# Set-up and plan moved into the mixer block, x loaded by halves, one stage order per engine, and a last stage that adds by DMA

## The reference, cut to what matters

```python
x = x + _layernorm(_L0_attn_ref(_layernorm(x), ...))
x = x + _layernorm(_L0_ffn_ref(_layernorm(x), ...))

# mixer
x = _lin(x, w1); x = silu(_depthwise_conv(x, conv_w, conv_b))
x_delta = softplus(_lin(x, dl_w, dl_b))
A_bar = exp(-x_delta * _lin(x, A_w, A_b))
A_cum = cumprod(A_bar, axis=1)
h = cumsum(_lin(x, B_w, B_b) * A_cum, axis=1)
ssm_out = _lin(h, C_w, C_b) + _lin(x, D_w, D_b)
out = ssm_out + _lin(ssm_out * silu(_lin(ssm_out, w2)), w3)

# ffn: top 2 of 8 experts for each token, and a shared one
probs = softmax(xn @ router_w); topv, topi = top_k(probs, 2)
for e in range(8):
    out = out + comb[:, e:e + 1] * _swiglu(xn, gate_up_w[e], down_w[e])
out = out + _swiglu(xn, shared_gate_up_w, shared_down_w)
```

## Time and profile before

| | us |
|---|---|
| median of 3 runs | 1341.65 |
| lowest and highest | 1341.48, 1345.4 |
| the profiled execution's own time | 1347.18 |
| its span in the trace | 1345.2 |
| PE, DVE, ACT, POOL busy | 1131.8, 858.6, 636.2, 310.0 |

### The profile page before, as it was taken

One profiled execution on the slowest core, in us unless ns is written; L12 is line 12 of the kernel. 1 busy time (PEld: TensorE's weight loads), 2 busy tenths in 40 slices (PEclk: granted clock), 3 DMA queues, 4 the chain that ended last, 5 costly groups with the idle time before them and its releaser, 6 DMA issues. The chain is left out here.

```text
span 1345.2 us, 23563 instructions
## 1 busy us (share of the span) xinstructions
PE 1131.8 (84%) x7568; PEld 998.5 (74%) x7568; DVE 858.6 (64%) x2158; ACT 636.2 (47%) x1275; POOL 310.0 (23%) x378
## 2 busy tenths in 40 slices
PE   1587888887897889829899999999999999999930
PEld 1365566665665646518899999999999999999930
DVE  3497589579868862515466666666666666666636
ACT  3545655555565433404344444444444444444414
POOL 2022025225322521320111111111111111111124
PEclk9798999899898989869999999999999999999975
DMA  5654647557474732235946811611111166211135
GB/s 184 220 186 157 225 155 247 180 181 265 154 244 153 248 118 67 87 145 227 320 110 214 331 31 31 219 31 28 28 24 30 31 212 208 48 31 31 31 93 172
DMA packets 96553, 191.71 MB, mean 143 GB/s; under 512 B 8704, under 2 KB 59392, under 8 KB 96512
## 3 DMA queue, kind: packets, MB, share of 16 engines
q1 hardware_dynamic: 82208, 172.48, 37.2%
...
## 5 line engine op out<-in xcount | busy, mean ns | idle before, releaser
L1162 PE MATMUL gu_ps<-xg_hi,w_ring 128*128 128x256 f32 x1248 | 356.8, 286 | 7.3 <-DMA w_ring<-w_split 7.3
L1164 PE MATMUL gu_ps<-xg_hi,w_ring 128*128 128x256 f32 x1248 | 348.4, 279 | 0.0
L1163 PE MATMUL gu_ps<-xg_lo,w_ring 128*128 128x256 f32 x1248 | 348.4, 279 | 0.0
L1134 POOL DMA_INDIRECT acc_scratch<-y,ids x78 | 127.3, 1633 | 587.0 <-DVE y L1234 560.7
L1255 DVE TENSOR_SCALAR gate<-gu_ps 128x256 f32<-128x256 f32 x312 | 132.1, 423 | 198.2 <-PE gu_ps L1164 198.2
L1215 ACT ACTIVATE gate<-gate 128x256 f32<-128x256 f32 x312 | 130.3, 418 | 243.1 <-DVE gate L1255 243.1
L1162 PEld LDWEIGHTS gu_ps<-xg_hi,w_ring 128*128 128x128 f32 x1248 | 236.1, 189 | 8.5 <-issue 5.7
L1163 PEld LDWEIGHTS gu_ps<-xg_lo,w_ring 128*128 128x128 f32 x1248 | 236.2, 189 | 0.0
L1164 PEld LDWEIGHTS gu_ps<-xg_hi,w_ring 128*128 128x128 f32 x1248 | 235.6, 189 | 0.0
L1207 ACT ACTIVATE hg_hi<-gate 128x256 fp32r<-128x256 f32 x312 | 129.9, 416 | 114.8 <-DVE gate L1262 114.8
L1173 PE MATMUL down_ps<-w_ring,hg_hi 128*128 128x256 f32 x624 | 175.3, 281 | 0.3 <-DVE hg_lo L1250 0.3
...
## 6 DMA issues: line engine op xcount, KB each, us to landing
...
```

The costliest lines, as they stand in the source:

```text
L1162: nc.tensor.matmul(out, e_hi[:, f, cols], xg_hi[:, par, c, :], start=c == 0, stop=False)
L1163: nc.tensor.matmul(out, e_hi[:, f, cols], xg_lo[:, par, c, :], start=False, stop=False)
L1164: i = nc.tensor.matmul(out, e_lo[:, f, cols], xg_hi[:, par, c, :], start=False, stop=c == DC - 1)
```

## The change

- The block `split_weights` is gone. Its loads, splits and constants are stages of `mixer`: p (weight splits), k (a bias sum), tab (tables on POOL). SP's queue begins with the two halves of x; the raw weights pass through the memory of `xnt`.
- x is loaded, measured, rooted and normalised by halves of 512 tokens (stages m, N), and the next batch's halves are loaded as soon as PE has transposed the last one's.
- Stages are cut finer: dl and A apart, scan into ac, bx and h, d 0 to 5 by output group on PE and ACT, the split of xs by channel half. The carries of both scans are copied by DVE where POOL did it.
- ORDER is now written out for all batches and the tail, word by word ("b6/1" is stage b of unit 6 in batch 1), for PE, ACT, DVE and POOL, and there is one for SP too. TAIL is gone. Six chunks of weights (w10 to w15 of the last batch) are split behind the last unit of that batch.
- The block `plan` is gone: its DVE instructions stand at the end of the mixer's DVE program, its eight clearing DMAs at the end of SP's.
- The block `finish` is gone: its stages stand at the end of `experts`. Behind group 2 SP copies x1 from DRAM to `out` in DRAM by four DMAs of 1 MB. At the end nobody adds on DVE: POOL issues for each chunk one DMA that adds the normalised 512 rows to `out` (accumulate).

```diff
-def split_weights(nc, weights, full, consts, w_hi, w_lo, w_full, vec, ident, zeros, ones, neg_half, tok_id, pad, tables):
...
-        @block.sync
-        def _(sp):
-            for n, (r, hi, lo, at, src, chunks) in enumerate(parts):
-                width = src.shape[1]
-                sp.dma_start(r[:, at:at + chunks * width].rearrange("p (c n) -> p c n", c=chunks),
-                             src.rearrange("(c p) n -> p c n", p=P)).then_inc(loaded[n], 16)
-            sp.dma_start(vec[:, :], consts).then_inc(vec_loaded, 16)
-            for at, src, chunks in full:
...
-def mixer(nc, x, w_e, w_s, shared, xs_dram, x1_dram, acc_dram, fill, w_hi, w_lo, w_full, vec, ident, tok_id, zeros, ones, neg_half):
+def mixer(nc, x, w_e, w_s, weights, full, consts, shared, xs_dram, x1_dram, acc_dram, fill, w_hi, w_lo, w_full, vec, ident,
+          tok_id, pad, zeros, ones, neg_half, tables, group_expert, group_change, group_row, group_code):
...
+        past = decay[:, 0, 0:(NG + 1) * E].rearrange("p (g e) -> p g e", e=E)
+        over = decay[:, 1, 0:E * MAXG].rearrange("p (e j) -> p e j", e=E)
+        unused, expert_f, passed_f, row_f = [decay[:, 1, (4 + i) * 48:(4 + i) * 48 + NG + 1] for i in range(4)]
...
+                "x0/1 n0/0 x1/1 n1/0 xr0/0 n2/0 n3/0 n4/0 spare/0 n5/0 n6/0 n7/0 n8/0 n9/0 n10/0 n11/0 n12/0 n13/0 n14/0 st0/0 "
...
-            def load_x(b):
-                sp.dma_start(x_in[:, :, :], x[b, :, :].rearrange("(t p) d -> p t d", p=P)).then_inc(x_loaded, 16)
+            def load_x(b, half):
+                sp.dma_start(x_in[:, half * HT:(half + 1) * HT, :], x[b, rows_of(half), :].rearrange("(t p) d -> p t d", p=P)
+                             ).then_inc(x_loaded[half], 16)
...
+            load_x(0, 0)
+            load_x(0, 1)
+            for n in range(2):
+                load_weights(raw_w, *weights[n], w_raw_loaded[n])
+            load_weights(w_full, *full[0], w_full_loaded[0])
+            sp.dma_start(vec[:, :], consts).then_inc(vec_loaded, 16)
+            for n in range(2, len(weights)):
+                load_weights(raw_w, *weights[n], w_raw_loaded[n])
+            for n in range(1, len(full)):
+                load_weights(w_full, *full[n], w_full_loaded[n])
             for at, src, chunks in shared:
                 sp.dma_start(w_sh[:, at:at + chunks * src.shape[1]].rearrange("p (c n) -> p c n", c=chunks),
                              src.rearrange("(c p) n -> p c n", p=P)).then_inc(w_sh_loaded, 16)
...
+            def spare_rows(b):
+                sp.wait_ge(consts_made, 2)
+                sp.dma_start(xs_dram[SPARE:SPARE + G, :].rearrange("(p m) d -> p (m d)", p=P), spare).then_inc(ends_cleared, 16)
+                sp.wait_ge(start_made, 1)
+                sp.dma_start(acc_dram[T:T + G, :].rearrange("(p m) d -> p (m d)", p=P), zeros[:, 0:GT * D]).then_inc(ends_cleared, 16)
+
+            def next_x(b, half):
+                passed(t1_done, (b - 1) * 4 + 2 * half + 2)
+                load_x(b, half)
+
...
+            def unit_product(b, n, at, bank, done):
+                half, j = UNITS[n]
+                cols = slice(half * HALF, (half + 1) * HALF)
+                if b == 0 and n == 0:
+                    pe.wait_ge(w_lo_ready, at // (DC * H) + 1)
+                for c in range(DC):
+                    if n == 0:
+                        pe.wait_ge(xs_lo_ready, b * DC + c + 1)
+                    i = product(banks[bank][:, :], W(w_hi, at, c, H, j * P), W(w_lo, at, c, H, j * P),
+                                xs_hi[:, c, cols], xs_lo[:, c, cols], c == 0, c == DC - 1)
+                i.then_inc(done, 1)
...
+            def x_moments(b, half):
+                tiles = slice(half * HT, (half + 1) * HT)
+                dve.wait_ge(x_loaded[half], b * 16 + 16)
+                moments(lambda t: x_in[:, half * HT + t, :], st[:, tiles, :], mv[:, tiles, :], HT, x_order, b * 2 + half + 1,
+                        a_aggr, b * 2 + half + 1, ve[:, tiles], 1.0, EPS, mv_ready)
+
...
+            def acum_unit(b, n):
+                half, j = UNITS[n]
+                first = half == 0
+                dve.wait_ge(abar_ready, b * NU + n + 1)
+                dve.wait_ge(bx_ready, b * NU + n + 2)
+                if n == 0 and b > 0:
+                    dve.wait_ge(s_stored[0][0], 16 * b)
+                if n > 0:
+                    dve.wait_ge(carried_a, b * HC + min(n, HC))
+                nc.vector.tensor_tensor_scan(a_cum[:, :], decay[:, n % 2, :], zeros[:, 0:HALF],
+                                             1.0 if first else carry_a[:, j:j + 1], ALU.mult, ALU.add).then_inc(acum_ready, 1)
+                if first:
                     dve.wait_ge(acum_ready, b * NU + n + 1)
-                    dve.wait_ge(b_done, b * NU + n + 1)
...
+            def h_unit(b, n):
+                half, j = UNITS[n]
+                first = half == 0
+                dve.wait_ge(bx_ready, b * NU + n + 3)
+                dve.wait_ge(h_lo_ready, b * NU + n + 1)
+                if n == 0 and b > 0:
+                    dve.wait_ge(sd_done, 2 * b)
+                if n >= HC:
+                    dve.wait_ge(carried_h, b * HC + j + 1)
+                nc.vector.tensor_tensor_scan(h[:, n % 2, :], ones[:, 0:HALF], bx[:, :],
+                                             0.0 if first else carry_h[:, j:j + 1], ALU.mult, ALU.add).then_inc(h_ready, 1)
+                if first:
+                    dve.wait_ge(h_ready, b * NU + n + 1)
+                    nc.vector.tensor_copy(carry_h[:, j:j + 1], h[:, n % 2, HALF - 1:HALF]).then_inc(carried_h, 1)
...
+            for b in range(B):
+                sp.dma_start(out[b, :, :], x1_dram[b, :, :]).then_inc(x1_copied, 16)
             with sp.Fori(0, (NG - 3) // 2) as i:
                 for k in range(2):
                     turn(i * 2 + 3 + k, 1 - k)
-            sp.wait_ge(x1_loaded, 16 * NC)
             for par in range(2):
                 sp.wait_ge(rows_loaded[par], 16 * (NG // 2 + 1))
+            sp.wait_ge(all_added, 1)
+            for c in range(NC):
+                sp.dma_start(acc[:, c, :, :], acc_dram[c * TC * P:(c + 1) * TC * P, :].rearrange("(t p) d -> p t d", p=P)
+                             ).then_inc(acc_loaded[c], 16)
+            sp.wait_ge(out_added, 16 * NC)
...
+            pool.sem_inc(all_added, 1)
+
+            def root(c):
+                pool.wait_ge(moments, c + 1)
+                nc.gpsimd.tensor_tensor(rs[:, c, :], ve[:, c, :], neg_half[:, 0:TC], ALU.pow).then_inc(rooted, 1)
+                pool.wait_ge(rooted, c + 1)
+                nc.gpsimd.tensor_tensor(nm[:, c, :], mv[:, c, :, 0], rs[:, c, :], ALU.mult).then_inc(rs_ready, 1)
+
+            def add_out(c):
+                if c == 0:
+                    pool.wait_ge(x1_copied, 16 * B)
+                pool.wait_ge(normed, c + 1)
+                nc.gpsimd.dma_start(token_rows(out)[c, :, :, :], acc[:, c, :, :], accum_op=ALU.add).then_inc(out_added, 16)
+
+            root(0)
+            for c in range(1, NC):
+                root(c)
+                add_out(c - 1)
+            add_out(NC - 1)
```

894 lines of the change are left out of this document (365 added, 529 removed), and 73 rows, old and new, of the table ORDER.

## The result

The changed kernel takes 1234.05 us (1232.97 to 1237.28) against 1343.53 for the kernel before on the same chip: a ratio of 0.9187, 95% interval 0.9166 to 0.9207. That is 109 us less. The forecast was 52 less, with a range that ended 34 us above what was measured.

What follows compares the result with a forecast made beforehand. The prediction saw a serial chain: start-up, four batches, tail, plan, experts, finish, with PE and DVE waiting for each other in the mixer. Its terms, -23 -5 -12 -6 -10 -2 +6, gave -52 us: 1341.65 to 1290, range 1268 to 1311.

Steps and rivals of the forecast that it cites:

- start: Set-up before batch 0's first unit product: x loads first, by halves, so that product comes at 34 instead of 57.4; -23 us.
- units of batch 0: From batch 0's first unit product to the next batch's `u`, 71 us before: the border's wait nearly covered; -5 us.
- two full periods: Mixer, from first product into `u` of one batch to the next, 120 us before: 6 less each, -12 us.
- batch 3 and tail: From the last `u` to PE's end, 212 us: six chunk splits moved to the tail, PE's work unchanged; -6 us.
- plan: Last scatter's issue to the experts' first rows, 20.7 us: one barrier remains, plan and clears run beside scatters; -10 us.
- copy of x1: Experts, behind group 2: four 1 MB copies replace eight loads that held SP for 13.18 us; -2 us.
- last stage: After the last add: loads start 3.8 us sooner, but POOL's eight adding DMAs, 3.4 us per issue, limit it; +6 us.
- the floor is PE's 103 of 120: Mixer periods: PE's busy 103 us of each 120 us period taken as the least a period could take.
- little more than the border's wait: Two full periods: 6 us saved each, where PE's longest single wait, at the batch's border for the last `bx`, was 5.6.
- the order gives much: Rival on the mixer's new order: periods near 108, tail -12, total 1272 us; chance 0.12.
- busy for 96 of 108: Sign against the rival of periods near 108: DVE would have to work 96 us of each.
- cheap adds: Rival on the last stage: POOL's issue price doesn't grow with the rows, 1.56 us, stage -4, total 1280; chance 0.17.

## Why the prediction was wrong, step by step

| step | forecast, bounds | measured |
|---|---|---|
| start | -23, -18 to -26 | -22.9 |
| units of batch 0 | -5, 0 to -8 | -9.5 |
| two full periods | -12, +4 to -30 | -27.0 |
| batch 3 and tail | -6, +4 to -16 | -35.7 |
| plan | -10, -5 to -13 | -8.2 |
| copy of x1 | -2, -5 to +9 | +1.3 |
| last stage | +6, -4 to +27 | -7.7 |
| sum | -52 | -109.7 |

The measured steps are differences of the marks in the two traces (34.51, 95.69, 202.87, 308.36, 484.2, 498.65, 1192.01, 1235.5 against 57.45, 128.15, 248.09, 367.77, 579.3, 601.95, 1294.01, 1345.2).

The step that failed most is "six chunk splits leave batch 3 for the tail, 6 x 0.995 = 6 us less on DVE [...] PE's work is the same". Two things are wrong in it.

First, it priced a split by its duration and left out what stands in front of it. The row that it used, also says that DVE stood idle for 66.1 us ahead of the 64 splits, more than they worked. The views of the periods were read for PE alone; DVE's own list, shown above, has 17.6 us of waiting for `e_high` in one batch of 120. The runs show what a split at the wrong place costs in the new order: all sixteen early 42 us, four of them 20, of which 11 to 15 are waits for the ring. They do not show that this was the whole gain. Without the ring's waits the kernel before gets 13 us faster, not 66, and in the traces its last stretch 7.8 us shorter, not 35.7. (The table shows it more exactly than the text on the change: in DVE's new order ten splits of the last batch, w6 to w15, stand behind its last `bx`, where three, w13 to w15, stood there before.)

Second, "the floor is PE's 103 of 120" and "PE's work is the same" took a busy time for a constant. It holds products at the lower clock, which a long wait brings with it (3.78 us against 1.98 for the same four). By the table above, 22 us less of idle time went with 13 less of busy time. In the periods, where PE's busy time fell by 1 and by 5 us, it was less.

The units of batch 0 came out at -9.5, a little outside their bounds, and the periods at -27.0, inside theirs and more than twice the forecast. There the prediction took "little more than the border's wait" and gave the finer stages no price of their own; in the new order gluing them again costs 29 to 53 us in these three stretches. The rival "the order gives much" had the right mechanism with periods near 108 (107.2 and 105.5 came) and a chance of 0.12, but it gave the tail -12. DVE "busy for 96 of 108" spoke against it; DVE turned out to be busy for 87 of 107 and 93 of 105 and could bear it, and in the first of these its own waits for `e_high` were gone.

Undoing all of the order costs 76 us; undoing its last part, moving the splits, or gluing dl to A costs 46, 42 and 43 each. The first two of these three lie in the last stretch and are two ways to spoil the same time, so they don't add up. The third lies mostly in the batches before it. Which single difference between the old and the new sequence of the batches 0 to 2 gives their gain was not settled, nor was the move of the carries' copies to DVE tried by itself.

In the last stage the unknown issue price was mis-sized: 3.4 taken, 1.33 measured (1.4 by POOL's pace), below even the lower end of 1.56, which was an indirect DMA's. With it the "cheap adds" case came true, though not by its own sum, and the agreement is partly luck. That case asked for -4; the stage took 7.7 less. It took 13.9 us from the last add's issue to the first normalised chunk, where 15.6 were reckoned, 7.1 until that chunk's add had landed, 18.6 for the seven other landings and 3.9 to the end. So the adds landed 2.7 us apart, where the sum took 3.6 for each transfer. It had reckoned with one packet at a time on each of the 16 engines; in the row from 1210 to 1225 the packets' times add up to 1.24 times what 16 engines have. Whether POOL's pace of 2.7 or the transfers set that distance is not shown. Against this stand the 3.6 us of POOL's DRAIN behind the last landing, a term that the prediction did not have. A packet's own time was 0.908 x 16 x 29.0 / 4224 = 0.100 us, against 0.110 for the indirect adds and 0.047 for plain ones.

The Trainium skill, page "DMA: Bandwidth & Descriptors", section "Anatomy of one DMA", says that making descriptors costs little; the trace agrees in the main, four times the rows in one DMA cost POOL 0.5 us more, and the case it spoke for is the one that came. The 3.2 us that the prediction worked out from that page for a whole add did not come: the adds landed 6.4 to 6.6 us behind their issue. The Trainium skill, page "Collectives: The Full Stack", section "The bandwidth ceiling", has an add at half the rate of a copy; the rows show a factor of 2.1 in the time of a packet.

The copy of x1 was forecast at -2 and came to +1.3, but both are differences of two large prices. The copies cost 8.1 us (693.4 to 685.3). The eight loads cost the same in the changed kernel (693.4 in the run that adds on DVE), so the exchange itself was worth nothing; the 692.1 of the kernel before leave 1.3 unexplained. The 4.8 us of the earlier trace rows were only the part that was shown as a wait for weights.

The start and the plan were right, in size and, where the trace shows it, in mechanism. ACT began to scale at 9.92 (8.8 forecast), the last copy of `u` was over at 23.24 (22.8), and the first product of a unit stood at 34.51 (34). One sum in it is off without effect: 4.6 us and the moments and root behind them give 7.9, not 8.5. The eight clears ran beside the scatters, as forecast.
